# Three of a transformer layer's transposes: on TensorE, or on VectorE by blocks of 32

## The chip, the cores and the metric

One core of one Trainium2 chip runs the whole kernel. The metric is the device time of one execution in microseconds (us); of several runs the median is given. The engines are TensorE (PE in the profile, with PEld for its weight loads), VectorE (DVE), ScalarE (ACT), GpSimd (POOL) and SyncE (SP, which here only issues transfers). All data are f32.

## The reference, cut to what matters

The input x has 8 batches of 512 tokens of 256 features. Each token goes through a transformer layer and then through a mixture of 8 experts, of which only the one that the token is closest to counts.

```python
out = norm1(x) @ (sf_w * mask).T + sf_b ; x = x + out
q, k, v = norm2(x) @ wq.T, ... @ wk.T, ... @ wv.T           # 16 heads of 16
att = relu(q @ k.T / 4) * causal ; att = att / (sum(att) + 1e-9)
x = x + (att @ v) @ wo.T + bo
x = x + relu(norm3(x) @ ff1_w.T + ff1_b) @ ff2_w.T + ff2_b   # 1024 wide
x = norm4(x0 + x)                                            # x0: the layer's input
assign = argmax(x @ centroids.T)                             # one of 8 experts
y = x + expert[assign](norm(x)) ; out = norm(x + alpha * y + (1 - alpha) * x)
```

A matrix product on TensorE needs its contraction on the 128 partitions. Tokens lie on the partitions when they are loaded or normalised, so before each product over features the tile of tokens by features has to be transposed.

## The kernel before, in words

The kernel goes through the 8 batches (`for b in range(NB)`), and then through the tiles of 128 tokens of the experts. Within batch b a software pipeline runs three batches at once: the attention of batch b, the feed-forward network of batch f = b-1, and the fourth norm, the affinities and the ranks of batch g = b-2. Each engine has its own program (`pe_batch`, `dve_batch`, `act_batch`, `pool_batch`, and the loop in `sp_program`), whose order is written out by hand; the engines meet at semaphores, and an engine goes through its own program strictly in order.

TensorE's order in batch b, b at least 2 (`pe_batch`): queries and keys (`pe_queries_keys`, L465 and L473), values (`pe_values`, L517), the transposes of the third norm's rows of f (`pe_ln3_T`, L407), and then 9 steps n = 0 to 8. A step begins with a piece of the scores (`pe_scores`, L545), in the PSUM banks 0 to 3. VectorE multiplies the part at the diagonal with the mask (`dve_scores`, L998), ScalarE then takes the relu of the rest (`act_scores`, L1531), and only when that is done may TensorE write the next piece. What TensorE does in the meantime is the rest of the step: products of weights and values at steps 3, 5 and 7 (`pe_weigh`, L569), and "units" of the feed-forward network by the table `UNITS`. Units 0 to 7 are the eight tiles of its first product (`pe_ffn1`, L598, in the banks 6 and 7 in turn, each taken out by ScalarE with `act_ffn1`, L1523); units 8 to 15 are halves of the second (`pe_ffn2`, L604). Unit 8 waits until all eight tiles of the first are taken out:

```python
def pe_ffn2(eng, b, t, half):
    if t == 0 and half == 0:
        eng.wait_ge(s_f1e, FM * b + FM)
```

ScalarE takes a tile out behind its relu of the same step, if its unit stands in that step.

There are four places with transposes on TensorE against an identity matrix (`con` in the profile). Each turns 128x128 blocks into PSUM, eight in all, and two copies bring them to SBUF:

- `pe_x_T` (L435) turns the next batch's input, four blocks ahead of unit 13 and four behind it, at step 8; ScalarE copies (L1485). `pe_sf` (L444) multiplies it.
- `pe_ln2_T` (L454) turns the second norm's rows at the end of a batch; ScalarE and VectorE copy with gain and shift (L1490, L967). The change leaves it.
- `pe_ln3_T` (L407 with `r2xhT` as input) turns the third norm's rows ahead of step 0; ScalarE and VectorE copy with gain and shift (L1516, L1066).
- `pe_ln4_T` (L407 with `x` as input) turns the fourth norm's rows behind step 0's scores; ScalarE and VectorE copy (L1564, L1079). `pe_affinity` (L629) and `pe_rank` (L665 to L669) use them, and a chain of small operations of VectorE (`dve_affinity`, `dve_rank`).

At the end of a batch come `pe_sf` for the next, `pe_proj_o` (L577) and `pe_ln2_T`, with the last units between them. VectorE adds what comes out of PSUM, makes the norms' statistics (L885, L892) and normalises (L898, L960); GpSimd makes the inverse standard deviations (L1749, L1751), sends the ranks to memory (L1792) and adds residuals (L1770, L1777, L1784, L1802).

In the tables `BUFFERS`, attention weights of steps 2 and 5 lie in the buffer that also holds the third norm's rows and the transposed rows of the second (`xhT`).

## Time and profile before

| | |
|---|---|
| median of 3 runs | 854.35 us (854.03 to 854.39) |
| the profiled execution's own time | 852.4 us |
| its span, first to last instruction | 850.6 us |
| TensorE busy | 832.7 us, 98% |
| VectorE, ScalarE, GpSimd busy | 456.6, 354.7 and 282.0 us |
| granted clock of TensorE over the span | 0.996 |
| a middle batch (2 to 6) | 69.7 us; the eight batches end near 550 us |

The times of the profile are of one execution, which was 1.95 us faster than the median; 1.8 us of it lie outside the span. A busy engine is one that has an instruction in it, and matrix products overlap, so the distance from the start of one group to the start of the next tells more of TensorE than a group's length.

### The profile page before, as it was taken

What the parts mean: (1) busy time and instruction counts of PE and PEld (TensorE: products, weight loads), DVE (VectorE), ACT (ScalarE), POOL (GpSimd) and SP (SyncE); (2) the same over time, 40 slices, a digit from 0 to 9 for tenths busy, and PEclk for the clock granted to TensorE, in tenths of its full rate; (3) what the DMA queues carried; (4) which work ended last, traced back from release to release, by engine and by line L of the source; (5) the groups of instructions that cost most, each with busy time, mean ns of one, the idle gap of its engine ahead of it and who ended that gap; (6) DMA issues with size and microseconds to landing.
All of it is one profiled execution on the core that took longest, in us unless ns stands there. A gap on an engine that the chain in (4) does not pass through costs nothing.

```text
span 850.6 us, 19429 instructions
## 1 busy us (share of the span) xinstructions
PE 832.7 (98%) x7394; PEld 558.2 (66%) x7394; DVE 456.6 (54%) x1334; ACT 354.7 (42%) x591; POOL 282.0 (33%) x392
## 2 busy tenths in 40 slices
PE   8999999999999999999999999999999999999994
PEld 5546576467467557547646655858999976776673
DVE  5475355257356445535628734633589555565652
ACT  1443424433432631542452253241433376677670
POOL 3503021332061052142225207124464445434422
PEclk9999999999999999999999999999999999999998
DMA  6500100020020020002003012415554798978930
GB/s 249 186 2 27 50 2 1 27 76 1 27 75 2 26 61 15 2 27 74 1 27 125 1 51 71 155 37 163 167 196 133 268 339 299 344 278 311 332 142 15
DMA packets 38593, 93.29 MB, mean 110 GB/s; under 512 B 13987, under 2 KB 26916, under 8 KB 30566
## 3 DMA queue, kind: packets, MB, share of 16 engines
q1 hardware_dynamic: 33206, 80.42, 26.8%
q0 software_dynamic: 4864, 11.10, 4.3%
q8 instruction: 59, 0.97, 0.5%
q10 hardware_dynamic: 432, 0.54, 0.3%
q14 instruction: 32, 0.26, 0.1%
HBM read 81.07 MB, written 11.23 MB: 109 GB/s over the span
## 4 chain that ended last, share of the span: by engine, by line
PE 92%; DVE 4%; POOL 1%; issue 1%; ACT 1%; DMA 1%; POOLq 0%; DVEq 0%; ACTq 0%
PE ps L598 14%; PE ps L604 12%; PE ps L691 10%; PE ps L709 9%; PE ps L545 9%; PE ps L569 7%; PE ps L755 4%; PE ps L731 4%; PE ps L517 3%; PE ps L577 3%; PE ps L444 3%; PE ps L465 3%; PE ps L473 3%; PE ps L407 2%; PE ps L677 1%
## 5 line engine op out<-in xcount | busy, mean ns | idle before, releaser
L604 PE MATMUL ps<-ff2T,hT 128*128 128x256 f32 x512 | 121.0, 384 | 0.2 <-ACT hT L1523 0.2
L598 PE MATMUL ps<-x3x,ff1T 128*128 128x512 f32 x256 | 118.8, 604 | 0.1
L1531 ACT ACTIVATE arena<-ps 128x1536 f32<-128x1536 f32 (+3 forms) x49 | 65.1, 1328 | 127.3 <-DVE arena L998 126.8
L604 PEld LDWEIGHTS ps<-ff2T,hT 128*128 128x128 f32 x512 | 94.4, 190 | 16.2 <-issue 3.4
L998 DVE SCALAR_TENSOR_TENSOR arena<-ps,arena 128x512 f32<-128x512 f32 (+4 forms) x59 | 44.8, 767 | 105.3 <-PE ps L545 63.2
L709 PE MATMUL ps<-w_sb,arena 128*128 x400 | 95.7, 383 | 0.0
L709 PEld LDWEIGHTS ps<-w_sb,arena 128*128 128x128 f32 x400 | 72.3, 190 | 15.9 <-issue 8.1
L598 PEld LDWEIGHTS ps<-x3x,ff1T 128*128 128x128 f32 x256 | 45.7, 190 | 52.1 <-issue 47.9
L545 PE MATMUL ps<-arena 32*128 32x512 f32 (+7 forms) x896 | 73.0, 434 | 1.8 <-ACT hT L1017 1.2
L545 PEld LDWEIGHTS ps<-arena 32*128 32x128 f32 x896 | 36.1, 184 | 37.2 <-issue 30.9
L1523 ACT ACTIVATE hT<-ps,col 128x512 f32<-128x512 f32 x64 | 43.8, 685 | 36.4 <-PE ps L598 35.8
L569 PE MATMUL ps<-arena 64*32 64x256 f32 (+7 forms) x1584 | 55.6, 399 | 0.0
L1839 POOL DMA_INDIRECT out_y<-arena,ids x34 | 35.2, 1036 | 58.4 <-DVE arena L1314 50.7
L1749 POOL TENSOR_TENSOR rs_ln<-mv_ln,eps 128x4 f32<-128x4 f32 x24 | 5.9, 246 | 145.9 <-DVE mv_ln L892 145.9
L691 PEld LDWEIGHTS ps<-arena 128*128 128x128 f32 x448 | 52.2, 192 | 0.7
L691 PE MATMUL ps<-arena 128*128 128x128 f32 x448 | 52.5, 275 | 0.0
L1790 POOL TENSOR_TENSOR spare<-spare 128x1 f32<-128x1 f32 x8 | 1.6, 205 | 150.8 <-PE ps L569 136.7
L1825 POOL DMA_INDIRECT arena<-token_store,ids x34 | 33.5, 984 | 53.6 <-DMA ids<-slot_table 45.2
L569 PEld LDWEIGHTS ps<-arena 64*32 64x32 f32 x1584 | 26.0, 106 | 34.3 <-issue 31.8
L1601 ACT ACTIVATE arena<-ps,arena 128x128 f32<-128x128 f32 (+2 forms) x72 | 25.1, 422 | 54.7 <-PE ps L677 54.7
L1833 POOL TENSOR_TENSOR ers<-ers,nhalf 128x1 f32<-128x1 f32 x68 | 38.8, 571 | 5.3
L1490 ACT ACTIVATE r2xhT<-ps,col 128x512 f32<-128x512 f32 x8 | 6.2, 777 | 81.2 <-PE ps L454 81.1
(231 smaller groups left out, 1579.3 us busy)
## 6 DMA issues: line engine op xcount, KB each, us to landing
arena<-in_w SPq DMA_DIRECT2D x27, 1024.0 KB, 6.8
hT<-in_w SPq DMA_DIRECT2D x16, 1024.0 KB, 7.6
wts<-in_w SPq DMA_DIRECT2D x9, 1024.0 KB
w_sb<-in_w SPq DMA_DIRECT2D x8, 1024.0 KB, 5.0
token_store<-x SPq DMA_DIRECT2D x8, 520.0 KB, 3.6
arena<-in_x SPq DMA_DIRECT2D x8, 512.0 KB, 3.8
arena<-in_epack SPq DMA_DIRECT2D x18, 134.0 KB, 5.2
slot_table<-padid POOLq DMA_DIRECT2D x4, 576.0 KB, 6.2
```

Source lines behind the costliest of these rows:

```text
L545: last = eng.matmul(ps[:, s, c:c + S - kt * KT], k[r, gt, kt, :, :].rearrange("p g c -> p (g c)"), q[r, gt, kt * KT:S], start=True, stop=True)
L569: last = eng.matmul(ps[32 * s:32 * s + 32, 4 + gp, kt * KT:S], vA[r, kt, 4 * gt + s, :], src[r, s, c:c + S - kt * KT], start=start, stop=s ...
L598: last = eng.matmul(ps[:, 6 + m % 2, :], ff1T[:, kd, m * P:(m + 1) * P], xT3[:, kd, :], start=kd == 0, stop=kd == KD - 1)
L604: last = eng.matmul(quarter(6, t), hT[:, m, t * P:(t + 1) * P], ff2T[:, m, :], start=m == 0, stop=m == FM - 1)
L691: last = eng.matmul(ps[:, b0 + f // 4, (f % 4) * P:(f % 4 + 1) * P], w1_ring[w1_of[j][0]][:, c:c + P], sxT[u][:, kd, :], start=kd == 0, st ...
L709: last = eng.matmul(ps[:, 4 + j % 2, 0:H], shT[u][:, f, :], w2_sb[:, bass.ds(at + f * H, H)], start=f == 0, stop=f == FM - 1)
L731: last = eng.matmul(ps[quarter_rows(q), b0 + i, :], sxT[u][:, kd, quarter_rows(q)], w1_ring[w1_of[j][PART_OF[q]]][:, c:c + S], start=kd == ...
L998: eng.scalar_tensor_tensor(out=o, in0=i, scalar=0.0, in1=mask[:, at:at + w].unsqueeze(1).broadcast_to([P, i.shape[1], w]), op0=ALU.max, op ...
L1523: eng.activation(hT[:, m, :], ps[:, 6 + m % 2, :], ACT.Relu, bias=col[:, C_F1B + m:C_F1B + m + 1]).then_inc(s_f1e, 1)
L1531: eng.activation(o, i, ACT.Relu).then_inc(s_sa, 1)
L1833: eng.tensor_tensor(srs[k][u][:, :], srs[k][u][:, :], nhalf[:, 0:1], ALU.pow).then_inc(p_rs[k], 1)
L1839: eng.indirect_dma_start(out=out, out_offset=bass.IndirectOffsetOnAxis(ap=ids[:, j:j + 1], axis=0), in_=oo[u], in_offset=None, bounds_chec ...
```

## The change: what it does

In the batches 2 to 7 VectorE transposes in place of TensorE, for the third norm of f = 1 to 6, for the fourth norm of g = 0 to 5 and for the input of the batches 2 to 7. VectorE's transpose turns blocks of 32x32 each in its place. For the two norms (`dve_turn_blocks`) there are 16 instructions each (`N_TURN`): each reads 32 partitions and eight blocks side by side, and writes them to 32 partitions, so that the blocks, too, get to where a transposed matrix has them. Eight of the third norm's stand ahead of the mask of step 0 (`TURN3`), and eight behind it; eleven of the fourth norm's stand behind the mask of step 3 (`TURN4`), five behind that of step 4. The gain and shift of the third norm are put on by ScalarE in SBUF (`act_gain3`, twice).

For the input, eight more transfers (`sp_load_blocks`) bring the tokens to `xp` with the blocks of 32 already in place (runs of 32 numbers), and two transposes over all 128 partitions finish it (`dve_turn_input`, step 4).

Room for these lies in the parts of the experts' weights (`w2_sb`) that are loaded last, and their loads are put later (`W2_LOADS`). The values are made behind the scores of steps 0 and 1 (`VALUES`), the first product's units start at step 2, the affinities and ranks go to steps 4 and 5 in bank 7, the fourth norm is made at steps 1 and 2, and the last four units go to the end of the batch and to the next batch's step 0. GpSimd's order changes with it. The other batches' transposes of these three kinds stay on TensorE. Lines with waits whose counts alone change, and the loads' waits, are left out of the diff here.

```diff
-UNITS = ((0,), (1, 2), (3, 4), (5,), (6, 7), (8, 9), (10, 11), (12,), (13,))
-UNITS1 = ((), (0, 1, 2)) + UNITS[2:]
+UNITS = ((), (), (0, 1), (2,), (3, 4), (5, 6), (7, 8), (9,), (10, 11))
+UNITS1 = ((), (0, 1), (2, 3), (4,), (5, 6), (7,), (8, 9), (), (10, 11))
+VALUES = (range(2), range(2, NKT))
+N_TURN = 16
+TURN3, TURN4 = 8, 11
...
...
                 eng.wait_ge(s_sd, masked(b - 1, STEPS - 1))
             elif n == 0:
                 eng.wait_ge(s_qe, 2 * b + 2)
-                eng.wait_ge(s_ke, 2 * b + 2)
-                eng.wait_ge(s_ve, 2 * b + 2)
+                eng.wait_ge(s_ke, 2 * b + 1)
+                if b == 0:
+                    eng.wait_ge(s_ve, 2)
             else:
...
...
                 eng.wait_ge(s_ke, 2 * b + 2)
             if w == 0 and b >= 2:
-                eng.wait_ge(s_pos, b)
+                eng.wait_ge(s_ve, 2 * b + 2)
             if w == FIRST[1]:
...
         def pe_ffn1(eng, b, m):
-            if m == 0:
-                eng.wait_ge(s_Te["ln3"], b + 1)
-                eng.wait_ge(s_Td["ln3"], b + 1)
+            if m == 0 and b in (0, NB - 1):
+                eng.wait_ge(s_Te["ln3"], 2 if b else 1)
+                eng.wait_ge(s_Td["ln3"], 2 if b else 1)
+            elif m == 0:
+                eng.wait_ge(s_x3a, 2 * b)
+            if m < 2 and b:
+                eng.wait_ge(s_r3, 2 * b - 1 + m)
+            if 0 < b < NB - 1 and m in (5, 7):
+                eng.wait_ge(s_afd if m == 5 else s_rkd, b)
             if m >= 2:
                 eng.wait_ge(s_f1e, FM * b + m - 1)
...
                 if b == 1 and n == 0:
...
                 if b == 0:
                     pe_ahead(eng, n)
                     continue
-                if n == 0 and g >= 0:
-                    pe_ln4_T(eng, g)
-                if n == 2 and g >= 0:
-                    pe_rank(eng, g)
-                if n == STEPS - 1 and more:
-                    pe_x_T(eng, b + 1, 0, 6)
-                    pe_ffn2(eng, f, 2, 1)
-                    pe_x_T(eng, b + 1, 1, 6)
-                    continue
-                if n == STEPS - 1:
-                    eng.wait_ge(s_r3, 2 * f + 1)
-                    slot_pe_x_T(eng, 0)
+                if b > 1 and n == 0:
+                    pe_ffn2(eng, g, NT - 1, 1)
+                if b > 1 and n < len(VALUES):
+                    pe_values(eng, b, 4, VALUES[n])
                 for k in (UNITS1 if b == 1 else UNITS)[n]:
                     pe_unit(eng, f, k)
-                if n == 0 and g >= 0:
-                    pe_affinity(eng, g)
+                if n == 4 and g >= 0:
+                    pe_affinity(eng, g, 7)
+                if n == 5 and g >= 0:
+                    pe_rank(eng, g, 7)
             for w in (AVS - 2, AVS - 1):
                 pe_weigh(eng, b, w)
-            if more and b:
+            if b == 0:
+                pe_values(eng, 1, 6)
+                pe_proj_o(eng, b)
+            elif more:
                 pe_sf(eng, b + 1)
+                pe_ffn2(eng, f, NT - 2, 0)
+                pe_proj_o(eng, b)
+                pe_ffn2(eng, f, NT - 2, 1)
+                pe_ln2_T(eng, b + 1)
                 pe_ffn2(eng, f, NT - 1, 0)
-            elif b:
+            else:
+                pe_ffn2(eng, f, NT - 2, 0)
+                pe_ffn2(eng, f, NT - 2, 1)
+                eng.wait_ge(s_r3, 2 * f + 1)
+                slot_pe_x_T(eng, 0)
                 pe_ffn2(eng, f, NT - 1, 0)
                 pe_ffn2(eng, f, NT - 1, 1)
                 eng.wait_ge(s_sa, STEPS * NB)
                 slot_pe_layer1(eng, 0, range(3))
-            if b == 0:
-                pe_values(eng, 1, 6)
-            pe_proj_o(eng, b)
-            if more and b:
-                pe_ffn2_part(eng, f, NT - 1, (4, 5))
-            if more and b:
-                pe_ln2_T(eng, b + 1)
-                pe_ffn2_part(eng, f, NT - 1, (6, 7))
+                pe_proj_o(eng, b)
...
+        def dve_turn_blocks(eng, dst, src, part):
+            blocks = src.rearrange("p t (k s i) -> p t k s i", k=KD, i=32)
+            turned = dst.rearrange("p k (t s i) -> p t k s i", t=NT, i=32)
+            for k in part:
+                r, c = k // 4, k % 4
+                last = eng.transpose(turned[32 * c:32 * c + 32, :, :, r, :], blocks[32 * r:32 * r + 32, :, :, c, :])
+            return last
+        def dve_turn_rows3(eng, f, part):
+            eng.wait_ge(s_xh["ln3"], f + 1)
+            eng.wait_ge(s_f1, FM * f)
+            last = dve_turn_blocks(eng, xT3, xh, part)
+            if part[-1] == N_TURN - 1:
+                last.then_inc(s_x3t, 1)
+        def dve_turn_rows4(eng, g, part):
+            eng.wait_ge(s_xh["ln4"], g + 1)
+            if g:
+                eng.wait_ge(s_af, g)
+            else:
+                eng.wait_ge(s_s, 2 * STEPS)
+            last = dve_turn_blocks(eng, x4B, x4[:, :, 0:H], part)
+            if part[-1] == N_TURN - 1:
+                last.then_inc(s_x4t, 1)
+        def dve_turn_input(eng, b):
+            eng.wait_ge(s_xp, 8 * 16 * (b - 1))
+            if b > 2:
+                eng.wait_ge(s_sf, 2 * b)
+            for kd in range(KD):
+                last = eng.transpose(xB[:, kd, :], xp[:, kd, :, :].rearrange("p c i -> p (c i)"))
+            last.then_inc(s_xB, 1)
         def dve_ln3_T(eng, b):
-            eng.wait_ge(s_T["ln3"], 2 * b + 2)
+            eng.wait_ge(s_T["ln3"], 4 if b else 2)
             if b:
                 eng.wait_ge(s_f1, FM * b)
...
-            if b != 1:
+            if b == 0:
                 dve_values(eng, b)
             if b > 1:
-                dve_ln3_T(eng, f)
+                dve_turn_rows3(eng, f, range(TURN3))
             for n in range(STEPS):
+                if n == 6 and g >= 0:
+                    dve_rank(eng, g, 7)
                 if b == 0:
                     dve_first_scores(eng, n)
                 else:
                     dve_scores(eng, b, n)
+                if b > 1 and n == 0:
+                    dve_turn_rows3(eng, f, range(TURN3, N_TURN))
+                if b > 1 and n == 1:
+                    dve_mean_var(eng, "ln4", dve_add_ffn(eng, g, 1))
+                    dve_values(eng, b, 4)
+                if g >= 0 and n == 3:
+                    dve_turn_rows4(eng, g, range(TURN4))
+                if g >= 0 and n == 4:
+                    dve_turn_rows4(eng, g, range(TURN4, N_TURN))
+                if b and more and n == 4:
+                    dve_turn_input(eng, b + 1)
                 if b == 0 and n in (1, 2):
                     dve_add_sf(eng, 1, (n - 1,), 6)
                 if b == 0 and n == 4:
...
                 if b == 1 and n == 0:
                     dve_ln3(eng, f)
                     dve_ln3_T(eng, f)
-                if n == 0 and g >= 0:
-                    dve_ln4_T(eng, g)
-                if n == 1 and g >= 0:
-                    dve_affinity(eng, g)
-                if n == 2 and g >= 0:
-                    dve_rank(eng, g)
+                if n == 5 and g >= 0:
+                    dve_affinity(eng, g, 7)
                 if n == 3 and b == 0:
                     dve_ln2(eng, 1)
                 if n == 5:
...
                     dve_turn_out(eng, b, 1)
                 if n == (5 if b else 8):
                     dve_context(eng, b, 0)
-                if n == 6 and more and b:
+                if n == 7 and more and b:
                     dve_ln1_stats(eng, b + 1)
-                if n == 7 and b:
+                if n == 8 and b:
                     dve_add_ffn(eng, f, 0)
                 if g == N_CUT - 1:
...
                 dve_ln2(eng, b + 1)
                 dve_ln2_T(eng, b + 1)
             dve_mean_var(eng, "ln3", dve_add_o(eng, b))
+            if not more:
+                dve_mean_var(eng, "ln4", dve_add_ffn(eng, f, 1))
             if b:
-                dve_mean_var(eng, "ln4", dve_add_ffn(eng, f, 1))
                 dve_ln3(eng, b)
...
+        def act_gain3(eng, f, kd):
+            eng.wait_ge(s_x3t, f)
+            eng.activation(xT3[:, kd, :], xT3[:, kd, :], ACT.Identity, bias=col[:, C_B3 + kd:C_B3 + kd + 1],
+                           scale=col[:, C_G3 + kd:C_G3 + kd + 1]).then_inc(s_x3a, 1)
...
                     act_keys(eng, 1, (1,), (7, 5))
                     act_ln3_T(eng, f)
-                if n == 0 and g >= 0:
-                    act_ln4_T(eng, g)
+                if b > 1 and n < KD:
+                    act_gain3(eng, f, n)
                 if b:
                     for k in (UNITS1 if b == 1 else UNITS)[n]:
                         if k < FM:
                             act_ffn1(eng, f, k)
+                        if k == 0 and g >= 0:
+                            act_ln4(eng, g)
             if more and b:
-                act_x_T(eng, b + 1, 1, 6)
                 act_ln2_T(eng, b + 1)
...
-                eng.wait_ge(s_av, AVS * b + len(VISITS[3]))
-                pool_scatter_ids(eng, g)
+                pool_rstd(eng, g, "ln4")
+                pool_shift4(eng, g)
             if b:
                 pool_residual2(eng, f)
                 pool_pre_b(eng, b)
             pool_pre2(eng, b)
-            if more:
+            if b == 0:
                 pool_rstd(eng, b + 1, "ln1")
                 pool_pre_a(eng, b + 1)
-                if b == 0:
-                    pool_empty_lists(eng)
-                pool_rstd_ln2(eng, b + 1)
+                pool_empty_lists(eng)
+            elif more:
+                pool_pre_a(eng, b + 1)
+                pool_rstd(eng, b + 1, "ln1")
             else:
                 for j in range(4):
                     slot_pool_gather(eng, j)
                 slot_pool_rstd(eng, 0, 0)
                 slot_pool_rstd(eng, 1, 0)
+            if g >= 0:
+                eng.wait_ge(s_av, AVS * b + AVS - 2)
+                pool_scatter_ids(eng, g)
+            if more:
+                pool_rstd_ln2(eng, b + 1)
             pool_rstd(eng, b, "ln3")
-            if b:
+            if not more:
                 pool_rstd(eng, f, "ln4")
                 pool_shift4(eng, f)
```

## Rows read from the trace of the kernel before

**Rows 1.** Windows: stretch, length, busy PE, PEld, DVE, ACT, POOL, clock, DMA.

```profile
341.45:411.17 69.72, 69.72 (x647) 43.22 (x646) 35.34 (x90) 26.83 (x32) 19.65 (x21) 1.00 0.10 32
```

**Rows 2.** Timeline, TensorE, batch 5's start: start, length, engine, line, output and inputs, count.

```profile
341.45 3.67 PE L465 MATMUL ps<-r2xhT,wts 128*128 128x512 f32 x8
...
348.49 3.71 PE L517 MATMUL ps<-wts,r2xhT 128*64 128x128 f32 x64
352.13 1.09 PE L407 MATMUL ps<-con,r2xhT 128*128 128x128 f32 x8
353.15 1.14 PE L545 MATMUL ps<-arena 32*128 32x512 f32 x8
354.22 1.09 PE L407 MATMUL ps<-con,x 128*128 128x128 f32 x8
355.15 1.88 PE L598 MATMUL ps<-x3x,ff1T 128*128 128x512 f32 x4
```

**Rows 3.** Timeline, TensorE, the later steps of the same batch.

```profile
367.19 1.15 PE L545 MATMUL ps<-arena 32*128 32x192 f32 x16
...
373.09 1.15 PE L545 MATMUL ps<-arena 32*128 32x256 f32 x16
374.16 1.12 PE L598 MATMUL ps<-x3x,ff1T 128*128 128x512 f32 x2
...
377.79 1.14 PE L545 MATMUL ps<-arena 32*128 32x512 f32 x8
...
392.15 1.99 PE L604 MATMUL ps<-ff2T,hT 128*128 128x256 f32 x8
...
395.15 0.66 PE L435 MATMUL ps<-con,arena 128*128 128x128 f32 x4
395.64 1.89 PE L604 MATMUL ps<-ff2T,hT 128*128 128x256 f32 x8
```

**Rows 4.** Groups by shape, VectorE's transposes: busy us, mean ns | idle before.

```profile
L1029 DVE STREAM_TRANSPOSE arena<-ps 128x512 f32<-128x512 f32 x32 | 21.0, 696 | 31.0 <-PE ps L569 31.0
...
L1045 DVE STREAM_TRANSPOSE arena<-arena 128x512 f32<-128x512 f32 x16 | 11.4, 711 | 0.5
...
L1083 DVE STREAM_TRANSPOSE affT<-ps 128x128 f32<-128x128 f32 x8 | 2.5, 308 | 5.2 <-PE ps L629 5.2
```

**Rows 5.** Timeline, VectorE, the same batch.

```profile
341.48 0.68 DVE L1052 TENSOR_TENSOR x3x<-ps,x3x 128x512 f32<-128x512 f32 x1
...
344.36 0.38 DVE L892 BATCH_NORM_AGGREGATE mv_ln<-st_ln 128x2 f32<-128x6 f32 x4
...
346.43 1.35 DVE L898 TENSOR_SCALAR r2xhT<-x3x,mv_ln,rs_ln 128x256 f32<-128x256 f32 x4
...
369.56 1.23 DVE L998 SCALAR_TENSOR_TENSOR arena<-ps,arena 128x1024 f32<-128x1024 f32 x1 [3.88 <-PE ps L569]
374.30 0.69 DVE L998 SCALAR_TENSOR_TENSOR arena<-ps,arena 128x512 f32<-128x512 f32 x1 [3.51 <-PE ps L545]
...
381.85 1.91 DVE L1034 TENSOR_SCALAR den<-arena 128x32 f32<-128x32 f32 x1
...
399.97 1.31 DVE L1029 STREAM_TRANSPOSE arena<-ps 128x512 f32<-128x512 f32 x2 [3.46 <-PE ps L569]
```

**Rows 6.** Timeline, ScalarE, the same batch.

```profile
354.82 1.67 ACT L1531 ACTIVATE arena<-ps 128x1792 f32<-128x1792 f32 x1 [1.22 <-DVE arena L998]
...
375.02 1.45 ACT L1531 ACTIVATE arena<-ps 128x1536 f32<-128x1536 f32 x1 [1.14 <-DVE arena L998]
376.37 0.68 ACT L1523 ACTIVATE hT<-ps,col 128x512 f32<-128x512 f32 x1
...
391.67 1.24 ACT L1531 ACTIVATE arena<-ps 128x1280 f32<-128x1280 f32 x1 [3.92 <-DVE arena L998]
```

**Rows 7.** Timeline, GpSimd, the same batch.

```profile
345.10 1.01 POOL L1751 TENSOR_TENSOR rs_ln<-rs_ln,nhalf 128x4 f32<-128x4 f32 x1
...
381.30 2.41 POOL L1784 TENSOR_TENSOR x3x<-arena 128x1024 f32<-128x1024 f32 x1
```

More of the change, by code:

```diff
@@ L428, in pe_x_T @@
             eng.wait_ge(s_x, 16 * (b + 1))
-            if b:
-                eng.wait_ge(s_r3, 2 * (b - 2) + 1)
-            if b and kd:
-                eng.wait_ge(s_xTe, 2 * b + 1)
             for t in range(NT):
@@ L440, in pe_sf @@
                 eng.wait_ge(s_const, 1)
-            eng.wait_ge(s_xTe, 2 * b + 2)
+            if b < 2:
+                eng.wait_ge(s_xTe, 2 * b + 2)
+            else:
+                eng.wait_ge(s_xB, b - 1)
+            src = xT0 if b < 2 else xB
             for t in tiles:
                 for kd in range(KD):
-                    last = eng.matmul(quarter(bank, t), xT0[:, kd, t * P:(t + 1) * P], sfT[:, kd, :], start=kd == 0,
+                    last = eng.matmul(quarter(bank, t), src[:, kd, t * P:(t + 1) * P], sfT[:, kd, :], start=kd == 0,
                                       stop=kd == KD - 1)
@@ L507, in pe_ahead, with pe_values @@
                 pe_ahead_head(eng, wkT, 0, 7, s_k)
-        def pe_values(eng, b, bank=0):
-            if bank:
+        def pe_values(eng, b, bank=0, tiles=range(NKT)):
+            if b == 1:
                 eng.wait_ge(s_qe, 2 * b + 1)
                 eng.wait_ge(s_ke, 2 * b + 1)
-            for t in range(NKT):
+            for t in tiles:
+                if b > 1 and t % 4 == 0:
+                    eng.wait_ge(s_ke, 2 * b + 1 + t // 4)
                 for kd in range(KD):
@@ L1479, in act_x_T @@
                 eng.wait_ge(s_v, 2 * b)
-            if b >= 2:
-                eng.wait_ge(s_av, AVS * (b - 1) + released(max(n for n in range(STEPS) if BUFFERS[n] == 2)))
-            if b >= 3:
-                eng.wait_ge(s_af, b - 2)
             eng.activation(xT0[:, kd, :], ps[:, bank, :], ACT.Copy).then_inc(s_xTe, 1)
```

114 lines of the change are left out of this document (74 added, 40 removed).

## The prediction, as made before the result was known

> **What bounds the kernel now.** I read the windows of one batch first. A middle batch lasts 69.72 us and TensorE has an instruction in it for all 69.72, at the full clock, 2.4 GHz; VectorE has 35.3, ScalarE 26.8, GpSimd 19.7 [rows 1]. So in the loop nothing but TensorE counts, as long as the others deliver in time. Then the timeline of TensorE, start to start, which gives what each group really takes: the eight transposes of the third norm hold it for 1.02 us (352.13 to 353.15), the eight of the fourth for 0.93 (354.22 to 355.15) [rows 2], and four of the input's for 0.49 (395.15 to 395.64), twice a batch [rows 3]. No gap stands between groups. Last, the timelines of VectorE and ScalarE, for the loop that each step runs: scores, mask, relu, next scores. TensorE's filler in a step must be as long as that chain.
>
> **What is removed.** 1.02 + 0.93 + 0.98 = 2.93 us a batch, six times: 17.6 us, the most that the change can give. Their copies on VectorE and ScalarE hid under TensorE and give nothing.
>
> **What a turn costs.** VectorE gets 32 turns of 256 columns a batch, and two of 512. No row shows a transpose of 32 partitions, nor one that changes partitions from one to the next. Its own transposes take 308 ns for 128 columns and 696 for 512 from PSUM, 711 within SBUF [rows 4]; a straight line gives 437 ns for 256, or 442 from the 711. The lower end is the overlap: two of 512 take 1.31 us together, so the second adds 0.61 [rows 5], and a turn would then cost about 0.35. The upper end is a turn that starts only behind the one before with some idle in between, about 0.47. I take 0.437 without overlap, because both partitions read and written change from turn to turn and no overlapped pair in the trace does that; it is nearer to the upper end. 34 transposes come to some 15 us, VectorE to about 49 of 68: the sum fits, so only the places matter. I call the time per turn h.
>
> The Trainium skill (VectorE: DVE Perf Modes, "Two Vector instructions with no wait between them") says that an instruction whose input or output starts in another group of 32 partitions than the last one's begins only when all earlier ones have finished. By it every turn is held and the sum stands as I make it below; without it the overlap rival further down would be the forecast. No row here shows it.
>
> **First place: ahead of and behind the mask of step 0.** Q is the start of the queries. TensorE is through queries and keys at Q + 7.04 (348.49 - 341.45), through scores 0 at + 8.11 (1.07, 353.15 to 354.22), then a half of the second product (about 1.8) and a quarter of the values (3.64 in all, 348.49 to 352.13), + 10.82, scores 1 (1.07), the other values (2.73), so scores 2 could start at Q + 14.62 [rows 2]. VectorE: the additions start 0.85 ahead of Q (now 0.03 behind, but 0.9 more of TensorE's work stands between), the statistics end 3.26 later (341.48 to 344.74), the inverse deviations 1.37 after that (to 346.11), the normalising takes 1.35: Q + 5.25 [rows 5, 7]. Then 16 turns with two masks among them (0.42 by the line of 0.69 and 1.23, and 0.69), relu 1 of 1.45, and some 0.14 of wake-ups: scores 2 may start at Q + 7.94 + 16h = 14.93. TensorE waits 0.31 in all (a part of it already ahead of scores 1, for relu 0 of 1.67 behind eight turns) [rows 6]. ScalarE's two gains (about 0.7 each) fit around the relus, and GpSimd is free there.
>
> **Second place: the fourth norm, steps 3 and 4.** From the start of scores 3, mask 3 begins at 2.37 (367.19 to 369.56; it waits for a buffer) and lasts 1.23; 16 turns and mask 4 (0.69) follow, wake-ups 0.1: the affinities may start at 4.4 + 16h = 11.39. TensorE is there at 5.90 + 1.07 + 3.63 = 10.60 [rows 3, 5]. It waits 0.79. The two input turns come behind and have until mask 5.
>
> **Third place: unit 8 right behind unit 7 in step 6.** Unit 8 waits for all eight tiles to be taken out, and ScalarE takes out the eighth only behind relu 6. From the start of scores 6: mask at 1.21 (373.09 to 374.30), about 0.2 later here because the rank's operations go first, relu 0.72 after the mask, taking out 1.35 after the relu's start, 0.68 long: 4.16 [rows 5, 6], wake-up 0.05. TensorE is through scores (1.07) and unit 7 (1.82, half of 374.16 to 377.79) at 2.89 [rows 3]. It waits 1.3, and nothing hides it; before, a step lay between these units.
>
> **Batch 1** has no unit in step 7. There relu 7 ends at 392.91 when TensorE has finished its products at 392.15 [rows 3, 6]: 0.8 once.
>
> **At nothing:** the affinities, ranks and values are only moved. GpSimd's scatter and residuals move to idle stretches. SyncE issues eight more transfers of short runs, behind the store of the batch before and ahead of a part of the weights; they have most of a batch until step 4, and that cover gone would cost their landing once. The late weights have until the first expert's second layer. Taking transposes out at the batch's end leaves the second norm's chain 0.7 us of room.
>
> **Sum.** A batch: -2.93 + 0.31 + 0.79 + 1.3 = -0.53; six times -3.2, batch 1 +0.8: -2.4 us. The profiled execution of 852.4 (span 850.6) would become 850.0; it was 1.95 below the median, so the median goes from 854.35 to 852.0.
>
> **Rivals.**
> *Turns overlap*, 0.35 each. Then the first two waits vanish (7.94 + 5.6 and 4.4 + 5.6 are both under TensorE's times) and 1.3 is left: six times -1.63, +0.8, -9.0: 845.4. For it speaks the pair of 1.31; against it the change of partitions. Chance 0.18.
> *VectorE becomes the bound* (the other side). With h = 0.47 scores 2 wait 0.84 and the affinities 1.32: six times +0.53, +0.8: +4.0, 858.3. Each 0.01 in h moves the time by 1.9 us, since 32 turns stand on the chain. It decides from h = 0.449, where the sum is nought, and from 0.458 a slowdown can be measured. For it: 0.442 is the line within SBUF, and small gaps between dependent operations are usual. Chance 0.27.
> *GpSimd's port.* GpSimd's additions of 2.4 us now lie beside the fourth norm's turns. One row shows VectorE shut out by such an addition: an operation on 32 columns took 1.91 and ended at 383.76, GpSimd's at 383.71 [rows 5, 7]. If turns are shut out likewise, two additions delay the affinities by some 5 us a batch: near 882. Against it: VectorE's statistics and reads of PSUM are not stretched. Chance 0.03. The Trainium skill (SBUF — State Buffer, "Who interferes with whom") says that one SBUF input outside the two-port modes takes no shared port; 711 ns for 512 columns is no two-port rate, so by the page this does not happen.
> *The change doesn't do what it says*: it does; TensorE's instructions of L407 and L435 go.
> The forecast, h from 0.42 to 0.444, has 0.42; the strip around nought, 0.444 to 0.458, has 0.10.
>
> **Range and chances.** The forecast's own range is 849 to 854. To leave no more than 2 in 10 out I reach from the overlap to just over the slow case: 844.8 to 859.5. A difference of under 0.2%, 1.7 us, can't be told from none here. Faster takes the overlap and most of the forecast, 0.50; same takes the strip and the rest of the forecast, 0.20; slower takes the slow case and the port, 0.30.
>
> **What would show it.** In the new profile: no L407 or L435 between batches 2 and 7; 32 transposes of 256 columns a batch, and their start-to-start distance, the number on which all hangs; TensorE idle ahead of scores 2, of the affinities and of unit 8, released by ScalarE, VectorE and ScalarE; a batch of 69.2 us. A batch of 68.1 means overlap, one above 69.9 means that VectorE bounds it. Wrong altogether would be an idle TensorE at a fourth place, the second norm's transposes above all.

## The result, and the profile after

| | before | after | ratio |
|---|---|---|---|
| time | 854.22 us (854.03 to 854.39, 4 runs) | 860.32 us (860.20 to 860.50, 4 runs) | 1.0072 [1.0054, 1.0089] |
| the profiled execution's span | 850.6 us | 858.5 us (its own time 860.26) | |

The kernel became 6.1 us slower, outside the range. The experiments below show that this figure belongs to one kind of chip. On two other chips, 8 and 9, the same program takes 850.6 us where the kernel before takes 852.2 to 852.4.

The profile after, in the lines that answer to those of before. First the middle batch by engine (columns as in [rows 1]); it lasts 70.28 us instead of 69.72, and TensorE is without an instruction for 2.5 of them:

```profile
341.93:412.21 70.28, 67.81 (x622) 40.93 (x621) 47.32 (x122) 25.58 (x30) 19.54 (x21) 1.00 0.14 39
```

Then TensorE's timeline in this batch (start, length, line, tile, count, idle time before and its releaser); L538 are the values, L568 scores, L592 the weighing, L629 and L635 the feed-forward's two products, L660 the affinities:

```profile
349.96 1.99 PE L635 MATMUL ps<-ff2T,hT 128*128 128x256 f32 x8
351.89 1.09 PE L538 MATMUL ps<-wts,r2xhT 128*64 128x128 f32 x16
353.05 1.20 PE L568 MATMUL ps<-arena 32*128 32x448 f32 x16
354.18 2.84 PE L538 MATMUL ps<-wts,r2xhT 128*64 128x128 f32 x48
357.18 1.15 PE L568 MATMUL ps<-arena 32*128 32x128 f32 x16 [0.16 <-ACT arena L1612]
...
367.79 1.15 PE L568 MATMUL ps<-arena 32*128 32x256 f32 x16
368.86 3.70 PE L629 MATMUL ps<-x3x,ff1T 128*128 128x512 f32 x8
373.33 0.64 PE L660 MATMUL ps<-w_sb,centT 128*32 128x128 f32 x16 [0.76 <-DVE w_sb L1103]
...
381.31 1.98 PE L629 MATMUL ps<-x3x,ff1T 128*128 128x512 f32 x4
384.31 1.99 PE L635 MATMUL ps<-ff2T,hT 128*128 128x256 f32 x8 [1.02 <-ACT hT L1604]
...
396.28 1.41 PE L592 MATMUL ps<-arena 64*32 64x128 f32 x44
398.14 1.07 PE L592 MATMUL ps<-arena 64*32 64x192 f32 x20 [0.46 <-issue]
399.15 3.72 PE L462 MATMUL ps<-wts,w_sb 128*128 128x256 f32 x16
```

The transposes of [rows 2] and [rows 3] are gone, and the three forecast waits stand where they were expected. Scores 1 and 2 start late: 1.16 us behind the first 16 values' start (351.89 to 353.05) and 3.00 behind that of the other 48 (354.18 to 357.18), where a version without these waits takes 1.03 and 2.77 (the third experiment below). The affinities wait for VectorE's turns (5.54 us from 367.79 instead of 1.07 + 3.63), and unit 8 for ScalarE (3.00 us from 381.31 instead of 1.82). The last lines show the one that was not forecast: 64 weighing products take 2.87 us, from 396.28 to 399.15, and in the middle of them TensorE waits for nothing that the profile shows.

VectorE's turns, as groups and in time (the form's count, busy time and mean ns of one; then start and length):

```profile
L1103 DVE STREAM_TRANSPOSE x3x<-r2xhT 32x256 f32<-32x256 f32 x96 | 41.8, 436 | 1.6
L1103 DVE STREAM_TRANSPOSE w_sb<-x 32x256 f32<-32x256 f32 x96 | 41.8, 435 | 1.3
...
```

```profile
347.29 3.58 DVE L1103 STREAM_TRANSPOSE x3x<-r2xhT 32x256 f32<-32x256 f32 x8
...
365.38 4.91 DVE L1103 STREAM_TRANSPOSE w_sb<-x 32x256 f32<-32x256 f32 x11
```

Eight take 3.58 us and eleven 4.91: 0.447 each, of which 436 ns are the instruction. They do not overlap. By the code, the partitions written (`32 * c`) change with every turn, those read (`32 * r`) only with every fourth.

### The profile page after: what moved, and what is told of

The parts are those of the page before. It is cut to its first block, busy times and chain, and to the rows that moved or that the text cites. A ratio compares the mean times of both kernels' runs of the same rounds, so it can differ in the third digit from the quotient of the medians.

```text
span 858.5 us, 19362 instructions
## 1 busy us (share of the span) xinstructions
PE 824.0 (96%) x7250; PEld 545.9 (64%) x7250; DVE 525.0 (61%) x1526; ACT 347.5 (40%) x579; POOL 281.4 (33%) x392
## 4 chain that ended last, share of the span: by engine, by line
PE 68%; DVE 20%; issue 5%; ACT 3%; POOL 1%; another core or an unknown queue 1%; DMA 1%; DVEq 0%; POOLq 0%; ACTq 0%
PE ps L635 11%; PE ps L731 10%; PE ps L749 9%; PE ps L629 6%; PE ps L568 6%; PE ps L592 5%; DVE x3x L1103 4%; PE ps L795 4%; DVE w_sb L1103 4%; PE ps L771 4%; PE ps L600 3%; PE ps L462 3%; ACT arena L1612 2%; DVE arena L1033 2%; DVE st_ln L920 1%
## 5 line engine op out<-in xcount | busy, mean ns | idle before, releaser
L635 PE MATMUL ps<-ff2T,hT 128*128 128x256 f32 x512 | 121.3, 385 | 7.0 <-ACT hT L1604 7.0
L629 PE MATMUL ps<-x3x,ff1T 128*128 128x512 f32 x256 | 119.8, 607 | 0.1
L635 PEld LDWEIGHTS ps<-ff2T,hT 128*128 128x128 f32 x512 | 94.3, 190 | 32.4 <-ACT hT L1604 12.2
L629 PEld LDWEIGHTS ps<-x3x,ff1T 128*128 128x128 f32 x256 | 45.5, 189 | 57.8 <-issue 50.1
L568 PE MATMUL ps<-arena 32*128 32x512 f32 (+7 forms) x896 | 73.0, 434 | 3.2 <-ACT hT L1052 1.4
L592 PE MATMUL ps<-arena 64*32 64x320 f32 (+7 forms) x1584 | 59.9, 400 | 2.5 <-issue 2.4
L568 PEld LDWEIGHTS ps<-arena 32*128 32x128 f32 x896 | 36.0, 184 | 34.1 <-issue 25.0
L592 PEld LDWEIGHTS ps<-arena 64*32 64x32 f32 x1584 | 27.0, 106 | 41.1 <-issue 38.9
L1906 POOL DMA_INDIRECT arena<-token_store,ids x34 | 33.6, 987 | 46.4 <-DMA ids<-slot_table 37.5
L1103 DVE STREAM_TRANSPOSE x3x<-r2xhT 32x256 f32<-32x256 f32 x96 | 41.8, 436 | 1.6
L1103 DVE STREAM_TRANSPOSE w_sb<-x 32x256 f32<-32x256 f32 x96 | 41.8, 435 | 1.3
```

Of the source, the lines that this page charges most:

```text
L568: last = eng.matmul(ps[:, s, c:c + S - kt * KT], k[r, gt, kt, :, :].rearrange("p g c -> p (g c)"), q[r, gt, kt * KT:S], start=True, stop=True)
L592: last = eng.matmul(ps[32 * s:32 * s + 32, 4 + gp, kt * KT:S], vA[r, kt, 4 * gt + s, :], src[r, s, c:c + S - kt * KT], start=start, stop=s ...
L629: last = eng.matmul(ps[:, 6 + m % 2, :], ff1T[:, kd, m * P:(m + 1) * P], xT3[:, kd, :], start=kd == 0, stop=kd == KD - 1)
L635: last = eng.matmul(quarter(6, t), hT[:, m, t * P:(t + 1) * P], ff2T[:, m, :], start=m == 0, stop=m == FM - 1)
L1103: last = eng.transpose(turned[32 * c:32 * c + 32, :, :, r, :], blocks[32 * r:32 * r + 32, :, :, c, :])
```

## Experiments

Each run's kernel before ran beside it. All but the last group ran on chips where that took 852.2 to 852.4 us; "a batch" is the distance of two starts of L483 in the middle of the program. The first four expectations count from 860.3 us, since the unaltered kernel had been measured only once by then; on these chips it takes 850.6, and it is the differences that compare.

**One part changed at a time** (kernel before: 852.28 us).

*The scatter earlier.* In batches 2 to 6 GpSimd's scatter goes ahead of the next batch's inverse deviations.

```diff
+                if g >= 0:
+                    eng.wait_ge(s_av, AVS * b + 5)
+                    pool_scatter_ids(eng, g)
                 pool_rstd(eng, b + 1, "ln1")
...
-            if g >= 0:
+            if g >= 0 and not more:
```

> In the changed kernel TensorE loses 1.0 us in each of the batches 2 to 6 in its last products of weights and values (2.87 us from their start to the next group's against 1.89 before), right behind GpSimd's four indirect transfers, which now lie at step 8. Here these four go ahead of the first norm's deviations in the batches 2 to 6, just behind the rank, at step 6. Theory 1 (the indirect transfers beside dense small products hold TensorE up): the gap of 1.0 us goes in five batches, 860.3 becomes 855.3. Rival (the gap comes from where TensorE's instruction stream is fetched anew, whatever GpSimd does): the gap stays, 860.3 within 1 us.

Measured: 850.66 us (11 runs), ratio 0.9983 [0.9974, 0.9992], a batch of 69.3 us, no idle time at the last weighing. Neither the 855.3 of the first theory nor the 860.3 of its rival came. By itself the missing stall looked like the cause found; but the next three did not have it either, and two of them keep TensorE's and GpSimd's programs as they are. Against the unaltered kernel's 850.6 the move gives nothing here.

*Unit 8 waits for one tile fewer.* It reads the first four hidden tiles and writes bank 6, which is free when the seventh is taken out; the eighth is waited for by the next unit, which reads it.

```diff
-            if t == 0 and half == 0:
-                eng.wait_ge(s_f1e, FM * b + FM)
+            if t == 0:
+                eng.wait_ge(s_f1e, FM * b + FM - 1 + half)
```

> Unit 8 reads only the first four tiles and writes bank 6, so here it waits for seven tiles to be taken out in place of eight, and unit 9 for all eight. Theory (the third place of the prediction, unit 8 waiting for ScalarE's eighth tile behind relu 6, is paid in full): its 1.18 us in each of the batches 2 to 6 and about 1.6 in batch 7 go, nothing else gets late since relu 6 ends ahead of unit 8's end: 860.3 - 7.5 = 852.8. Rival (scores 7 then wait for relu 6 or VectorE's chain instead): less than 2 us are won.

Measured: 842.31 us (4 runs), ratio 0.9886 [0.9871, 0.9901], a batch of 68.0. Against 850.6 that is 8.3 us less, for 7.5 forecast. The wait ahead of unit 8 is gone; those ahead of scores 2 (0.15) and of the affinities (0.76) are unchanged.

*Turns that stay in their quarter of the partitions.* This version leaves out the moves of blocks from one quarter to another, so its products are of other numbers; it is there for the time alone. A turn reads and writes the same 32 partitions, and both change with every fourth turn.

```diff
-            r, c = k // 4, k % 4
-            last = eng.transpose(turned[32 * c:32 * c + 32, :, :, r, :], blocks[32 * r:32 * r + 32, :, :, c, :])
+            c, r = k // 4, k % 4
+            last = eng.transpose(turned[32 * c:32 * c + 32, :, :, r, :], blocks[32 * c:32 * c + 32, :, :, r, :])
```

> The 16 turns of each norm are ordered and placed so that source and target partitions of a turn are the same 32, and change only with every fourth turn; the blocks land in wrong places, so that the feed-forward products and the affinities are of other numbers. Theory (a turn in other partitions than the last one's starts only when that one has ended; the page's rule): of the 16 distances of 0.447 us some 12 fall to about 0.35, a group of 16 gets 1.2 us shorter, the waits ahead of scores 1 and 2 (0.5 us a batch) go and that ahead of the affinities (0.84) goes too: 6 times 1.3, 860.3 - 8 = 852.3. Rival (0.447 is what such a transpose takes, wherever it lies): no change, 860.3.

Measured: 843.45 us (4 runs), ratio 0.9898 [0.9883, 0.9914], a batch of 68.11. Its turns, and TensorE at the places of before:

```profile
L1103 DVE STREAM_TRANSPOSE w_sb<-x 32x256 f32<-32x256 f32 x96 | 34.6, 406 | 0.4
L1103 DVE STREAM_TRANSPOSE x3x<-r2xhT 32x256 f32<-32x256 f32 x96 | 34.0, 404 | 0.6
```

```profile
344.85 1.09 PE L538 MATMUL ps<-wts,r2xhT 128*64 128x128 f32 x16
345.88 1.20 PE L568 MATMUL ps<-arena 32*128 32x448 f32 x16
347.01 2.84 PE L538 MATMUL ps<-wts,r2xhT 128*64 128x128 f32 x48
349.78 1.15 PE L568 MATMUL ps<-arena 32*128 32x128 f32 x16
...
365.10 0.64 PE L660 MATMUL ps<-w_sb,centT 128*32 128x128 f32 x16
...
376.09 1.99 PE L635 MATMUL ps<-ff2T,hT 128*128 128x256 f32 x8 [1.02 <-ACT hT L1604]
```

96 turns keep VectorE busy for 34.0 us instead of 41.8: 0.354 each where one in four changes its partitions, 0.435 where all do. The waits ahead of scores and affinities are gone, and unit 8's is as it was; against 850.6 that is 7.2 us less, for 8 forecast. One more reading is possible: that it costs time to read in one quarter and write in another, and not to change quarters from turn to turn. The traces answer it. In this version no turn does the former, and still a turn behind a change starts 0.013 us after the one before it has ended (0.403 to 0.452 from start to start), while the others start 0.063 or more before that (0.326 to 0.373). In the changed kernel the turns that read and write the same quarter are held like all others (0.445 to 0.450).

*The turns in other places*: 6, 7 and 3 of the third norm's (the last ones and both gains at step 1), 2, 7 and 7 of the fourth's.

```diff
-                dve_turn_rows3(eng, f, range(TURN3))
+                dve_turn_rows3(eng, f, range(6))
...
+                if g >= 0 and n == 3:
+                    dve_turn_rows4(eng, g, range(2))
```

> Same turns, other places: the third norm's 6 ahead of mask 0, 7 behind it, 3 behind mask 1 (both gains then behind relu 1); the fourth norm's 2 ahead of mask 3, 7 behind it, 7 behind mask 4. Theory (the waits ahead of scores 1 and 2 and ahead of the affinities come from where the turns stand in VectorE's order, not from its load of 48 of 70 us): 0.5 + 0.8 us a batch go, 0.2 may come back ahead of scores 3: 860.3 - 6.5 = 853.8. Rival (VectorE as a whole is the bound of these steps): the waits only move, 860.3 within 1.5.

Measured: 850.66 us (11 runs), ratio 0.9981 [0.9972, 0.9990], a batch of 69.24. Nothing waits at the scores, but the affinities now wait 1.05 instead of 0.76. Of the 6.5 us that the theory forecast nothing came; it went as the rival has it, the waits only moved.

**Again, and together** (kernel before: 852.25 us).

*The changed kernel itself.*

> The changed kernel, nothing altered. In its profile TensorE stood about 1 us in every batch at the last product of weights and values ahead of the gathered rows' affinities, with nothing that the profile shows to wait for (2.87 us from one such product to the next where the kernel before takes 1.89), and lost 2.1 us more behind the last attention output of the program. None of the four variants so far shows it. Theory 1 (it belongs to that load of the program or to that chip, not to the change): here the stall is missing, and the time is about 852.3 - 2 = 850 to 851 us. Theory 2 (it belongs to the changed program's own timing, and each variant shifted that): it is there again, 858 to 860.5 us.

Measured: 850.60 us (850.41 to 850.95, 11 runs), ratio 0.9982 [0.9973, 0.9991], a batch of 69.3, the stall missing. A third time, on chip 9:

> The changed kernel, nothing altered, a third time. The first measurement gave 860.32 us with 1 us of stall per batch that nothing in the profile explains; the second gave 850.6 us without it. Theory 1 (the stall was that of one load or one chip, and rare): 850.4 to 851 us, no stall. Rival (it comes in about every second load): 858 to 860.5 us.

850.62 us (11 runs), ratio 0.9979 [0.9970, 0.9988]. Its batch, where the three waits are the only ones:

```profile
338.48:407.78 69.30, 67.30 (x622) 40.81 (x621) 47.31 (x122) 25.56 (x30) 19.52 (x21) 1.00 0.14 39
```

*63 more waits ahead of TensorE's first product.*

```diff
-            eng.wait_ge(s_warm, 1)
+            for _ in range(64):
+                eng.wait_ge(s_warm, 1)
```

> The changed kernel with 63 more waits, all met already, ahead of TensorE's first product: its whole later program lies further back in memory, and nothing else differs. Theory 1 (the stall ahead of the gathered affinities is one of fetching TensorE's instructions, which falls on a fixed place of its program): it is missing here or stands at another product, 850 to 860 us. Theory 2 (it hangs on the chip or on the load, not on the place): it behaves as in the unaltered kernel of this same call. Theory 3 (GpSimd's scatter stalls it): it is there at the same product.

Measured: 852.75 us (11 runs). TensorE's first product starts 3.45 us later (4.91 for 1.46); idle time behind it takes up a part, and the third batch's start is 1.68 us later (132.07 for 130.39). The batches are those of the unaltered kernel. No stall was there to move, so it tells nothing of one.

*Three edits at once* (unit 8, the cuts, the scatter), and the same without the scatter's move:

> The changed kernel with three edits at once: the last product of the feed-forward's first half-unit waits for one eviction fewer (the second half waits for the last), the two groups of turns are each cut in three, and the scatter is issued ahead of the next batch's reciprocal roots. Alone, these gave 842.31, 850.66 and 850.66 us. Theory 1 (each works on a wait of its own, so they add): the one wait is worth 8.3 us; the cuts moved the waits ahead of the scores to the affinities, so they add nothing: 842 to 843 us. Rival (with unit 8 on time, VectorE's turns are the last thing TensorE waits for, and the cuts give the 0.5 us per batch of the two scores' waits back): 839 to 840 us.

> As the kernel with three edits, but the scatter stays where the change has it. Theory 1 (the scatter's place costs TensorE nothing, since the variant that moved it alone and the one that did not move it both took 850.66 us): the same as with all three, within 0.5 us. Rival (the scatter holds TensorE at the last products of weights and values): 4 to 6 us slower than with all three.

Measured: 842.05 and 841.94 us (4 runs each), a batch of 67.95 in both, for 68.0 with unit 8's edit alone. The cuts add next to nothing as long as the affinities wait (1.05 in each batch), and the scatter's place costs nothing here.

**The affinities later** (kernel before: 852.41 us). Their products go behind the scores of step 5; in the second kernel the turns are cut as well.

```diff
                 pe_scores(eng, b, n)
+                if n == 5 and g >= 0:
+                    pe_affinity(eng, g, 7)
...
-                if n == 4 and g >= 0:
-                    pe_affinity(eng, g, 7)
```

> The changed kernel with the feed-forward's first half-unit waiting for one eviction fewer (alone 842.31 us, a batch of 68.0 us), and with the affinities' products issued behind step 5's scores (1.14 us) instead of ahead of them. The affinities waited 0.76 us for the fourth norm's turns in each of six batches. Theory 1 (the turns are ready 0.76 us late and nothing else is near): a batch of 67.2 to 67.3 us, 837.6 to 838 us. Rival (VectorE has become the bound there: what it does behind its turns, the one-hot and the numerators' turns, moves with the affinities and holds TensorE at the next weighing or at the ranking): 841 to 843 us, with a new wait in step 5 or 6.

> As the kernel before it, with both groups of turns cut in three (6, 7 and 3 of the third norm's, 2, 7 and 7 of the fourth's). With the affinities in their old place the cuts only moved 0.43 us of waits ahead of the scores to the affinities (1.05 us there, a batch of 67.95 us, 841.94 us). Theory 1 (those 1.05 us fit under step 5's scores, 1.14 us): no wait is left, a batch of 66.9 us, 835.5 to 836 us. Rival (VectorE is the bound): within 1 us of the kernel without the cuts.

Measured: 837.56 us (5 runs, ratio 0.9827 [0.9814, 0.9841], a batch of 67.22) and 835.63 us (5 runs, ratio 0.9803 [0.9790, 0.9816], a batch of 66.88). Both came as their theories forecast. In the second TensorE has no gap in the loop, as in [rows 1], but 2.84 us less to do:

```profile
331.19:398.07 66.88, 66.88 (x622) 40.89 (x621) 47.37 (x122) 25.72 (x30) 19.57 (x21) 1.00 0.15 41
```

*The kernel before, again.*

> The kernel before, nothing altered: its first measurements gave 854.35 us, and beside the variants it took 852.25 us. Theory 1 (its first profile held a smaller stall of the same kind, in the 0.27 us that its last batch was longer and elsewhere): a span of about 838.4 - 2 = 836.4 us from the first product to the last, with batches of 69.72 us all alike. Rival (the 2 us lie ahead of the first product or behind the last): the same 838.4 us between them.

One run of 852.20, batches of 69.72, 838.17 us to the end of the last product (838.37 in its first profile). So that profile held no stall: it was of an execution that took 852.4, and the 2 us are only in the timed runs of 854.35.

**On a chip of the other kind** (chip 5; kernel before: 854.39 us, 13 runs; the others ran on chips 8, 9 and 11).

> The changed kernel, nothing altered, a fourth time. Theory 1 (the first measurement's stall hung on the chip that it ran on: there the kernel before also took 854.22 us and not 852.3): 850.4 to 851 us wherever the kernel before takes 852.3, and 858 to 860.5 where it takes 854. Rival (it hangs on the load of the program, on any chip): 858 to 860.5 us beside a kernel before of 852.3.

> The changed kernel with the scatter of batches 2 to 6 ahead of the next batch's reciprocal roots. Where the stall shows beside it in the unaltered kernel: theory 1 (GpSimd's scatter, at 392.54 to 397.4 in the first profile, stalls TensorE's products at 396.28 on that chip) 850.5 to 853 us; rival (another cause) 858 to 860.5 us. Where no stall shows, 850.4 to 851 us and nothing is told apart.

> The version with no wait left in the loop (unit 8's wait, the affinities behind step 5's scores, both groups of turns cut in three), again, as 835.63 us before. Theory 1 (it stands on any chip): 835.4 to 836 us. Rival (on a chip with the stall it has it too): 841 to 846 us.

| | chips 8, 9, 11 | chip 5 | ratio on chip 5 |
|---|---|---|---|
| kernel before | 852.3 us | 854.39 us | |
| changed kernel | 850.6 (chips 8, 9) | 859.81 (4 runs) | 1.0063 [1.0046, 1.0079] |
| with the scatter earlier | 850.66 (chip 11) | 855.73 (10 runs) | 1.0017 [1.0007, 1.0027] |
| no wait left in the loop | 835.63 (chip 9) | 846.04 (4 runs) | 0.9906 [0.9889, 0.9922] |

GpSimd's scatter and the last weighing of batch 5 in the changed kernel on chip 5:

```profile
392.18 1.03 POOL L1872 DMA_INDIRECT slot_table<-toki,posi  x1 [0.17 <-issue]
393.51 0.97 POOL L1872 DMA_INDIRECT slot_table<-toki,posi  x1 [0.30 <-issue]
394.79 0.95 POOL L1872 DMA_INDIRECT slot_table<-toki,posi  x1 [0.30 <-issue]
396.04 0.96 POOL L1872 DMA_INDIRECT slot_table<-toki,posi  x1 [0.30 <-issue]
```

```profile
395.92 1.41 PE L592 MATMUL ps<-arena 64*32 64x128 f32 x44
397.77 1.08 PE L592 MATMUL ps<-arena 64*32 64x192 f32 x20 [0.44 <-issue]
```

The same on chip 9: the scatter stands in the same place against the products, and they run through.

```profile
392.95 0.96 POOL L1872 DMA_INDIRECT slot_table<-toki,posi  x1 [0.30 <-issue]
```

```profile
392.83 1.96 PE L592 MATMUL ps<-arena 64*32 64x128 f32 x64
```

The end of the stop can be placed. GpSimd's fourth instruction is over at 397.00, and the packets of its transfer move later. In 40 slices of 0.025 us from 397 to 398, on chip 5:

```profile
GB/s 0 0 0 0 0 0 0 0 0 0 0 0 0 0 0 0 0 0 0 0 0 0 0 0 8 2 4 4 2 1 1 0 0 0 0 0 0 0 0 0
```

The last of them has ended at 397.78, and TensorE goes on at 397.77. So it is in the batches 2 to 6 of all three profiles with the stall and the scatter in its place (the first one, and on chip 5 the changed kernel and the best version): in 15 of 15 TensorE goes on within 0.05 us of the fourth transfer's last packet. No packet of instructions moves around this stop (the one before starts at 391.12, the next at 404.95), which speaks against TensorE waiting for its own program. On chip 9 the packets end at 394.68, in the same place against the products, and nothing waits for them.

With the scatter earlier, on chip 5 (its four transfers at 379.39 to 384.20), the products run through there too; in the last batch the weighing that lies beside the gathered tokens' transfers (L1906) still stops:

```profile
393.49 1.96 PE L592 MATMUL ps<-arena 64*32 64x128 f32 x64
...
510.86 1.67 PE L592 MATMUL ps<-arena 64*32 64x192 f32 x30
513.19 1.13 PE L592 MATMUL ps<-arena 64*32 64x320 f32 x18 [0.67 <-issue]
```

```profile
507.60 1.03 POOL L1906 DMA_INDIRECT arena<-token_store,ids  x1 [1.10 <-issue]
508.94 0.96 POOL L1906 DMA_INDIRECT arena<-token_store,ids  x1 [0.30 <-issue]
510.20 0.95 POOL L1906 DMA_INDIRECT arena<-token_store,ids  x1 [0.30 <-issue]
511.45 0.95 POOL L1906 DMA_INDIRECT arena<-token_store,ids  x1 [0.30 <-issue]
```

The 855.73 us lie outside both ranges of the second expectation, 850.5 to 853 and 858 to 860.5. Its rival, another cause, fails for the batches 2 to 6 and stays possible for the rest. A batch falls from 70.28 to 69.44 us, where the other chips have 69.30; the 0.14 that are left are lost in a weighing again, the one beside the packets of the moved scatter (2.00 us from 384.84 to 386.84, for 1.86 in the unaltered kernel on the same chip). The third expectation's rival came true: the best version has the stall too (batches of 67.84, 846.04 us, the top of its range), and is still 8.4 us faster than the kernel before on that chip.

Last, both together, which was meant for such a chip but met one where the kernel before takes 852.30:

> The version with no wait left in the loop, and the scatter of batches 2 to 6 ahead of the next batch's reciprocal roots. Theory 1 (the scatter holds TensorE only on a chip like the one where the kernel before takes 854.3 us): beside a kernel before of 852.3 us it takes 835.4 to 836 us, the same as with the scatter in its old place; beside one of 854.3 us it takes 841 to 842, where the version without the move took 846.04. Rival (the move brings a wait of its own): 837 or more on the first kind of chip.

835.71 us (4 runs), ratio 0.9804 [0.9787, 0.9820]: the move costs nothing there. What it gives on chip 5 in this version was not measured. The kernel before ran beside it once more:

> The kernel before, nothing altered. Theory 1 (what it loses on the chip with the stall lies in the expert part behind the last attention output, where GpSimd's gathers and scatters run): on such a chip 296.6 us from the last output product to the end instead of 294.64 and batches of 69.72; on another kind of chip 294.64.

852.12 us, 294.62 us from the last output product to the end: no answer on where it loses its 2 us on chip 5.

## Why the prediction was wrong

**The step that failed** is one line of "At nothing": GpSimd's scatter moves to an idle stretch. The stretch was idle for GpSimd, but it runs into TensorE's last weighing, 64 products with 64 loads of weights in 1.89 us; its last transfer starts 0.12 us behind the first of these products. On chip 5 they stop for about 1 us each time. The kernel before has its scatter, from 371.68 to 376.49 in its trace, beside scores and a unit of eight large products (L598 at 374.16 in [rows 3]) and no weighing. From the changed kernel's traces on chip 5 and on the others: the five distances from batch 2 to batch 7 add 5.02 us (351.71 for 346.69), the last batch, up to its last output product, 2.22 (67.02 for 64.80, most of it at the weighing beside the gathers, L1906), the part behind it 2.59 (297.21 for 294.62), 9.8 in all; the measured difference is 859.81 - 850.6 = 9.2. The kernel before is 2.1 slower there than on the others, so 7.1 us are the change's, against a gain of 1.7. This is the "idle TensorE at a fourth place" that the prediction named as what would make it wrong, and it gave it no price and no chance. The chip of the first measurement isn't recorded; the same stalls at the same places in its profile and its 854.22 us for the kernel before match chip 5.

The experiments show that the scatter's place makes the stall in the batches 2 to 6, and that the chip decides whether there is one. TensorE goes on when the fourth transfer's packets have landed. They don't show by what path a transfer holds it, nor what differs in the chip: the wait has no releaser in the profile. For the 4.8 us in the last batch and behind it, of which the kernel before loses 2.1 too, no run moved anything.

**The rest of the sum came out near, in part by luck.** Without the stall the profiled execution was forecast at 850.0 us; it took 850.45. The turn was 0.011 us longer than forecast; by the prediction's own 1.9 us for each 0.01 that alone would have taken most of the gain away (2.1 of 2.4). It didn't, because other terms erred the other way. Term by term, in the trace without the stall:
- Removed, 2.93 us a batch: the version with no waits has a batch of 66.88, 2.84 less than 69.72.
- A turn, 0.437 forecast, 0.447 to 0.449 measured, 436 ns of it the instruction. It was the number on which all hung, and it came out within 0.002 of the 0.449 from which the forecast's sum turned to a loss. The reason given for no overlap was half right: the partitions written change with every turn, those read only with every fourth; one of the two is enough. The Trainium skill (VectorE: DVE Perf Modes, "Two Vector instructions with no wait between them") says that a change of the group of 32 partitions holds an instruction back until the earlier ones have finished. The experiment that kept the group in three of four turns agrees: 0.354 for 0.435, and each turn behind a change is held though none there reads in one group and writes in another.
- First place, 0.31 forecast, 0.36 measured: scores 2 start 15.24 us behind the queries (338.48 to 353.72), and 14.88 where nothing waits (334.90 to 349.78 in the third experiment). VectorE's chain was 0.3 longer than forecast, 0.18 of it by the longer turn, but TensorE's own work was 0.26 longer too (14.88 for 14.62).
- Second place, 0.79 forecast, 0.83 measured. The longer turn would make 0.97 of it, so the terms beside it were 0.14 too high.
- Third place, 1.3 forecast, 1.18 measured as a wait; without it a batch is 1.29 shorter (69.30 to 68.01), and the time 8.3 us (850.6 to 842.31).
- Batch 1, 0.8 forecast; 0.74 measured, ahead of a scores group at 110.71 and released by ScalarE.

The waits came to 2.42 a batch (69.30 less 66.88) for 2.40 forecast. What was mis-sized is the removal, 2.84 for 2.93: 0.5 us over six batches, most of what the gain of 1.7 lacks to 2.4. In the prediction's listed terms the first place's 5.25 adds up to 5.13 only (-0.85 + 3.26 + 1.37 + 1.35); measured, the turns start 5.36 behind the queries (341.93 to 347.29).

**The rivals.** Overlap was forecast to give 9.0 us with a batch of 68.1; the kernel that has most of it gave 8.8 with one of 68.11. So the arithmetic of that rival was right and its condition wrong. VectorE as the bound was priced by h = 0.47; h came out at 0.447 to 0.449, at the edge from which it decides. The port of GpSimd took nothing: the eleven turns at 365.38 run at 0.446 each beside GpSimd's additions. The Trainium skill (SBUF — State Buffer, "Who interferes with whom") says so of VectorE's instructions with one SBUF input outside the two-port modes, and the trace agrees.

A second error is one of reading. The profiled execution was 1.95 us faster than the median, and I added the 1.95 to the forecast as if it were a constant of every run. The runs show two levels of the kernel before, 852.3 and 854.4, by chip; a program's profile at the one level says nothing about what is added at the other.

## What to carry to other kernels

A gap of this size between a profile and the median of its runs is a warning that the profile may come from another chip than the runs, and that terms which it prices at nothing may cost there. When turns or other helpers of a second engine are put on the chain, list every consumer in order of time and remove its wait by moving the consumer, not by cutting the helper into pieces: the cuts alone gave nothing (850.66 for 850.6), the two moved waits 13.0 us (850.6 to 837.56), and only behind them the cuts gave 1.9 more. Keep runs of indirect transfers away from TensorE's densest stretches of small products; in this kernel the move costs nothing where it isn't needed and gives 4.1 us where it is (855.73 for 859.81).

## What was unexpected of the hardware

Four indirect transfers of GpSimd, 0.96 to 1.03 us each, make a run of 64 small products about 1 us longer on one chip (5). On two others (8 and 9) they do nothing to it, with the same program and the same place of both to within 0.1 us, and on chip 11 no version with both in these places has the stall either. Where it is, it ends within 0.05 us of the landing of the last transfer's packets. Two transposes of 32 partitions one behind the other cost 0.447 us each when the partitions written change from one to the next, with 0.013 us between instructions of 436 ns; where neither those read nor those written change, the next one starts 0.063 us or more before the first has ended. 63 waits that are met already put TensorE's first product off by 3.45 us (4.91 for 1.46), 55 ns each; 1.68 us of it are left at the third batch.
